# VectorE's loops run two expert rounds or two images per turn, and its statistics rounds are written out

## What is computed

```
x = x + attention(ln(x))                        # 16 images
t = t + mixture_of_experts(ln(t))               # 8 experts, 4096 tokens, all experts computed
x = x + grouped_conv3x3(ln(x))                  # 16 images
t = t + rk4(ln(t)[:, 0])                        # t[:, 0] of each image, 255 steps in a row:

def _mlp(y): h = tanh(W1 y + b1); h = tanh(W2 h + b2); return W3 h + b3     # 128 -> 512 -> 512 -> 128
k1 = f(y); k2 = f(y + dt/2*k1); k3 = f(y + dt/2*k2); k4 = f(y + dt*k3)
y  = y + dt*(k1 + 2*k2 + 2*k3 + k4)/6
```

## Time and profile before

| | us |
|---|---|
| median of three runs | 2901.73 |
| profiled execution, time | 2900.79 |
| profiled execution, span | 2899.0 |
| VectorE busy | 2371.2 |
| TensorE busy | 2813.0 |
| ScalarE busy | 1551.6 |
| expert rounds (64) | about 191 to 1577 in the span |
| statistics rounds (8) | about 1589 to 1762 |
| image rounds (16) | about 1762 to 2112 |
| output and plain steps | about 2112 to 2897 |

### The profile page before, as it was taken

One profiled execution on the slowest core, in us unless ns is written; L12 is line 12 of the kernel. 1 busy time (PEld: TensorE's weight loads), 2 busy tenths in 40 slices (PEclk: granted clock), 3 DMA queues, 4 the chain that ended last, 5 costly groups with the idle time before them and its releaser, 6 DMA issues.

```text
span 2899.0 us, 208902 instructions
## 1 busy us (share of the span) xinstructions
PE 2813.0 (97%) x82250; PEld 2411.6 (83%) x82250; DVE 2371.2 (82%) x13418; ACT 1551.6 (54%) x10124; POOL 737.0 (25%) x1417
## 2 busy tenths in 40 slices
PE   7789999999999999999999999999999999999999
PEld 3468888888888888888888887888889999999998
DVE  4668888888888888888888887888878888888887
ACT  5445556555555555555555444444445555555555
POOL 5023323323323333233232000111112222222222
PEclk8779999999999999999999999999999999999999
DMA  3000000000000000000000000000000000000000
GB/s 117 0 8 16 11 11 14 11 11 14 11 11 14 11 12 13 11 14 11 11 14 8 1 0 1 0 0 0 0 16 0 0 0 0 0 0 0 0 0 14
DMA packets 21983, 28.21 MB, mean 10 GB/s; under 512 B 4385, under 2 KB 12897, under 8 KB 21545
## 3 DMA queue, kind: packets, MB, share of 16 engines
q1 hardware_dynamic: 21928, 27.48, 3.2%
HBM read 25.24 MB, written 2.23 MB: 9 GB/s over the span
## 4 chain that ended last, share of the span: by engine, by line
PE 92%; DVE 4%; ACT 2%; issue 1%; DMA 0%; SPq 0%; DVEq 0%; ACTq 0%; POOLq 0%; POOL 0%
PE PSUM L675 22%; PE PSUM L681 20%; PE PSUM L862 17%; PE PSUM L736 12%; PE PSUM L666 5%; PE PSUM L858 4%; PE PSUM L838 2%; PE PSUM L843 2%; DVE PSUM L1367 1%; PE PSUM L773 1%; PE PSUM L702 1%; ACT HA L1050 1%; PE PSUM L706 1%; PE PSUM L743 1%; PE PSUM L513 1%
## 5 line engine op out<-in xcount | busy, mean ns | idle before, releaser
L1367 DVE TENSOR_REDUCE PSUM<-PSUM 128x32 f32<-128x64 f32 x2912 | 623.6, 232 | 99.3 <-PE PSUM L681 52.5
L675 PEld LDWEIGHTS PSUM<-HA,RL 128*128 128x128 f16 x11648 | 396.8, 96 | 205.0 <-ACT HA L1050 194.8
L1051 ACT ACTIVATE PSUM<-PSUM 128x32 f32<-128x32 f32 x2912 | 561.0, 194 | 0.0
L1050 ACT ACTIVATE HA<-PSUM 128x32 f16<-128x32 f32 x1456 | 288.9, 199 | 467.6 <-DVE PSUM L1367 467.5
L1050 ACT ACTIVATE HB<-PSUM 128x32 f16<-128x32 f32 x1456 | 289.1, 200 | 466.9 <-DVE PSUM L1367 466.9
L675 PE MATMUL PSUM<-HA,RL 128*128 128x16 f16 x11648 | 511.8, 170 | 15.4 <-ACT HA L1050 7.6
L675 PE MATMUL PSUM<-HB,RLU 128*128 128x16 f16 x11648 | 511.2, 170 | 4.8 <-ACT HB L1050 0.2
L420 POOL TENSOR_TENSOR G<-G 128x512 f16<-128x512 f32 x256 | 296.1, 1157 | 684.6 <-ACT G L1023 684.6
L681 PE MATMUL PSUM<-HA,RH 128*128 128x32 f16 x11648 | 465.0, 177 | 0.0
L681 PE MATMUL PSUM<-HB,RHU 128*128 128x32 f16 x11648 | 464.3, 177 | 0.0
L675 PEld LDWEIGHTS PSUM<-HB,RLU 128*128 128x128 f16 x11648 | 393.5, 96 | 47.9 <-ACT HB L1050 2.4
(11 more groups left out here) (309 smaller groups left out, 6982.0 us busy)
## 6 DMA issues: line engine op xcount, KB each, us to landing
G<-scores SPq DMA_DIRECT2D x64, 256.0 KB, 3.2
N<-in_x SPq DMA_DIRECT2D x8, 256.0 KB, 4.8
NHL<-in_w SPq DMA_DIRECT2D x1, 2048.0 KB, 10.3
STF<-in_w SPq DMA_DIRECT2D x1, 2048.0 KB, 14.7
out<-W2HL SPq DMA_DIRECT2D x8, 256.0 KB, 2.4
G<-in_r SPq DMA_DIRECT2D x1, 1024.0 KB, 5.5
R1K<-in_r SPq DMA_DIRECT2D x1, 256.0 KB, 2.8
R3F<-in_r SPq DMA_DIRECT2D x1, 256.0 KB, 5.7
```

What stands on the lines that cost most here:

```text
L675: mm(out[m // 2][:, 2 * B * (m % 2):2 * B * (m % 2) + B], lo[:, k, m], src[:, k, 0], start=False, stop=False)
L1050: A(hi[:, 2 * h:2 * h + 2, 0], src, ACT.Tanh, scale=1.0 / scale).then_inc(rk_hi, 1)
L1051: A(full, src, ACT.Tanh, scale=1.0 / scale).then_inc(rk_f, 1)
L1367: v.tensor_reduce(bank[:, SUM:SUM + 2 * B].rearrange("p (m b) -> p m b", m=2), bank[:, 0:4 * B].rearrange("p (m c b) -> p m b c", m=2, c=2 ...
```

## The change

`rounds` gets a further argument `per`, the number of rounds per turn. The body of the loop is repeated `per` times, with `i = n * per + alone + r`. The `alone = (count - 1) % per` rounds that are left over come first, outside the loop, with constants for thresholds. The experts have count 64 and per 2: one round outside, and 31 turns of two. The statistics have count 8 and per 7: none outside, and a loop that runs once. The images have count 16 and per 2: one outside, and 7 turns of two. No arithmetic, no order of operations on any engine and no other engine's program is changed.

```diff
-            def rounds(start, count, beside):
+            def rounds(start, count, per, beside):
+                alone = (count - 1) % per
                 part(start, beside(0, True), 0, EDGE)
-                with dve.Fori(0, count - 1) as i:
+                for i in range(alone):
                     part(start + 2 * i, beside(i, False), EDGE, SLOTS)
                     part(start + 2 * (i + 1), beside(i + 1, False), 0, EDGE)
+                with dve.Fori(0, (count - 1) // per) as n:
+                    for r in range(per):
+                        i = n * per + alone + r
+                        part(start + 2 * i, beside(i, False), EDGE, SLOTS)
+                        part(start + 2 * (i + 1), beside(i + 1, False), 0, EDGE)
                 part(start + 2 * (count - 1), beside(count - 1, False), EDGE, SLOTS)
-            rounds(1, GROUPS, experts_beside)
+            rounds(1, GROUPS, 2, experts_beside)
             moe_tail(step, expert)
-            rounds(S_STAT, NT, lambda t, opening: lambda slot: statistics(t, slot))
-            rounds(S_CONV, B, lambda t, opening: lambda slot: conv(t, slot))
+            rounds(S_STAT, NT, 7, lambda t, opening: lambda slot: statistics(t, slot))
+            rounds(S_CONV, B, 2, lambda t, opening: lambda slot: conv(t, slot))
```

## The result

The changed kernel takes 3003.53 us (3003.05 to 3004.06, 4 runs) beside 2901.22 us before: a ratio of 1.0354, with a 95% interval of 1.0341 to 1.0367. It is slower by 102 us. Its profiled execution has a span of 3002.1 us.

A forecast was written before the change was run, and what follows sets the result against it. A ring through three engines including VectorE and TensorE was taken to bound the kernel. 2900.8 + 74.5 (refetching turns) - 0.5 - 0.7 + 2.2 = 2976.3 us, plus 0.9 for the median: 2977, range 2896 to 3018.

The forecast's parts named there:

- The old turn at 0.105 us: Experts' loop before the change: each branch taken costs 0.105 us; 32 turns fewer were to save 3.4 us.
- The count of blocks: Experts' loop after the change: some 312 instructions from 419, touching four blocks, five with the block ahead.
- rival (3): Images' loop is 12 instructions longer than counted and touches four blocks too: about 16 us more, 2993 us, chance 0.15.
- Four blocks as the limit: VectorE's code store holds four blocks of 128 instructions; a fifth replaces the first, so every turn back refetches.
- The hold of 2.0 us: At each of 30 experts' turns, VectorE waits 2.0 us for the target's code, all of it exposed.
- The bounds of 1.1 and 3.2: Lower and upper price in us of refetching code at an experts' turn; they gave totals of 2941 and 3018 us.
- The landing of a 2 KB load: Nearest row in size, 1.7 us, from which the price of refetching 8 KB at an experts' turn was taken.
- Three borders at 0.2 us each: Experts' loop: three more block borders crossed per turn with a load each, 0.6 us per turn.
- Straight code at +2.2 us: Written-out rounds add about 1420 instructions, 11 borders at 0.2 us each: +2.2 us.
- (1): Store is larger or the block ahead doesn't push out the loop's first: nothing reloads, -2.4 us, 2899 us, chance 0.27.
- (2): Code is kept, borders cost nothing and a removed turn was dearer, 0.17 us: 2894 us, chance 0.08.

The follow-up runs named there:

- the test of the edge: The changed kernel with 100, 106 and 94 tiny memsets more at the head of VectorE's program: 3040.3, 3011.0 and 2897.5 us.
- The shifts: The changed kernel with 60, 32, 100, 106 or 94 memsets more at VectorE's program head: 2897.23, 2917.96, 3040.3, 3011.0 and 2897.5 us.
- the target named in advance: The changed kernel with the loop option hint_back_edge, one instruction naming the block of the turn's target to the prefetcher: 2900.43 us.
- the kernel shifted by 60: The changed kernel with 60 tiny memsets more at the head of VectorE's program, moving all its code by 60 instructions: 2897.23 us.
- the one shifted by 32: The changed kernel with 32 tiny memsets more at the head of VectorE's program: 2917.96 us.

## Why the prediction was right, and what it mis-sized

The direction, the place and the mechanism came as forecast: 2977 us with a range of 2896 to 3018, measured 3003.5.

- **The old turn at 0.105 us: right.** With the 62 turns written out the stage fell by 6.5 us, which is 62 x 0.105. But a longer body doesn't keep that price. The turn of two rounds costs 0.145 us when it is kept.
- **The count of blocks: right.** The body has 312 instructions in the compiled program, and its head is at 418, one from my 419. It touches four blocks, and moving it into three removed the loss. The borders are two instructions earlier than I placed them, which mattered only in the test of the edge. The images' loop starts 76 behind a border by my count, 78 in truth, and has 298 instructions: it had 8 to spare and not 12, and rival (3) was closer than I thought.
- **Four blocks as the limit: right, on thin ground.** I called it the weakest step. The comparison with TensorE's blocks was no evidence, and no row could tell four blocks from five, so that it came right was in part luck. The shifts and the target named in advance are. The Trainium skill's 32 KiB (page "Runtime: NRT & Kernel Launch", section "Instruction fetch mechanics") agree with four blocks of 8 KB; its refill by 16 KiB blocks doesn't hold for this queue.
- **The hold of 2.0 us: too small.** The turn slot grew by 2.68 us against a plain one, where I had 2.0 + 0.1: 30 x 0.6 = 18 us more. The bounds of 1.1 and 3.2 held. The landing of a 2 KB load was the wrong neighbour. A packet of 0.3 to 0.5 us comes about 1 us behind the branch, and another 1.3 us pass until the next instruction.
- **Three borders at 0.2 us each: the wrong item.** They cost 0.14 us per turn, not 0.6, and show at two places, not at three. What stands in their place is the clock, 0.89 us per turn or 27 us in all. The prediction said that nothing here depends on the clock, because it was 1.00 in the earlier trace rows. That was true of the kernel before. The change itself made the idle time that brings the clock down, and this step I never took. 0.9 + 0.1 instead of 0.6 is 13 us more.
- **Straight code at +2.2 us: wrong in size.** Statistics and tail became 0.7 us faster, and 50 borders in the written-out experts cost some 1.5 us together. I took 0.2 us for every border from the earlier trace rows, two places where one shows. Most borders fall where the slot has slack; few cost that much.
- 18 + 13 less 2 is 29 above the 75 of the forecast: 104, where 102 were measured.

Of the rivals, (1) is what happens once the code lies well: -2.0 us in the runs of the kernel shifted by 60, where I had -2.4. (2) didn't occur. The turns were indeed dearer than read, but the new ones, not the old. (3) didn't occur in the changed kernel, but in the one shifted by 32, at 19 us against my 16.

## What to carry to other kernels

A loop body has a place as well as a length. Before an engine's loop is unrolled, count its instructions, registers and branch among them, and where its head lies between the borders. The sign of a body that doesn't fit is packets on a code queue in every turn, with a hole behind the branch that the profile puts down to "issue". If a loop stands just over the edge, move the code, name the target in advance, or write the rounds out; here, writing them out was best. And any hold of a few microseconds in a ring that includes TensorE has to be priced with what its clock does afterwards.

## What the runs showed of the hardware

- VectorE's code comes in 8 KB packets, 128 instructions each. The other code queue has 16 KB packets, 36 of them before, after and with everything written out; by its pace, one packet every 4 to 5 us in a stage's first round, it is TensorE's. VectorE keeps four blocks of 128 instructions; the load of the block ahead takes the place of the oldest.
- A taken branch to a block that is gone: one packet about 1 us behind it, and 2.8 us until the next instruction. With two or four instructions left in the target's block, a second hold of 2.0 to 2.2 us follows. Where the branch itself is the first instruction of a new block, that block's successor and the target are fetched together, and the hold leaves VectorE idle for 3.96 us.
- A hold of about 3 us in VectorE, with or without a load of code, lets TensorE's granted clock fall from 1.00 to 0.50, 2.5 to 5.3 us behind the branch, for 3 to 7 us, and costs 0.89 us beyond the hold itself.
- Fifty new blocks in straight code with constant thresholds cost about 1.5 us together (64 rounds at 21.56 instead of 21.54 us), half of it at three of the borders.
